# Graph and expert layers on one core: counts clamped by a tensor_scalar with a column of constants, one-hots made in pieces of four chunks

## What is computed

```
H   = l2_normalize_rows(layernorm(x))
XW  = H @ W_gcn
src, dst = edges and one self loop for each node
deg = segment_sum(ones, dst);  dinv = rsqrt(maximum(deg, 1e-30))
z_local  = segment_sum(XW[src] * (dinv[src] * dinv[dst])[:, None], dst) + b_gcn
z_global = 0.1 / n * (H @ (H.T @ H) @ W_V)
x = x + l2_normalize_rows(relu(z_local + z_global))
```

## Time and profile before

| what | us |
|---|---|
| median of 3 timed runs (5673.95 to 5677.72) | 5675.14 |
| the profiled execution, its own time | 5700.08 |
| its span, first to last instruction | 5698.0 |
| TensorE matmul busy in it | 4359.2 |
| VectorE busy | 3235.9 |
| ScalarE busy | 2114.7 |
| POOL busy | 1202.7 |

### The profile page before, as it was taken

One profiled execution on the slowest core, in us unless ns is written; L12 is line 12 of the kernel. 1 busy time (PEld: TensorE's weight loads), 2 busy tenths in 40 slices (PEclk: granted clock), 3 DMA queues, 4 the chain that ended last, 5 costly groups with the idle time before them and its releaser, 6 DMA issues. The chain is left out here.

```text
span 5698.0 us, 58897 instructions
## 1 busy us (share of the span) xinstructions
PE 4359.2 (77%) x18640; PEld 2870.1 (50%) x18640; DVE 3235.9 (57%) x6106; ACT 2114.7 (37%) x4158; POOL 1202.7 (21%) x1467
## 2 busy tenths in 40 slices
PE   1447355996784988879998898998787596889477
PEld 1335244775111767767775222223576465666366
DVE  7867244114897559731115898995787245453423
ACT  0003122113783045522223887888555011111222
POOL 1566666650220001000000111110010210000142
PEclk9868777997787989979998898899898798999788
DMA  8204243116443745320001443443453235462276
GB/s 351 103 1 162 93 134 88 39 38 208 158 155 113 241 167 196 117 45 0 0 0 58 157 156 124 165 159 94 164 191 128 88 109 177 148 199 90 107 221 203
DMA packets 460063, 733.30 MB, mean 129 GB/s; under 512 B 114081, under 2 KB 258974, under 8 KB 453004
## 3 DMA queue, kind: packets, MB, share of 16 engines
q1 hardware_dynamic: 410012, 690.18, 36.8%
q0 software_dynamic: 30096, 19.30, 1.2%
q10 hardware_dynamic: 19680, 20.48, 1.1%
HBM read 587.26 MB, written 147.21 MB: 129 GB/s over the span
## 5 line engine op out<-in xcount | busy, mean ns | idle before, releaser
L1459 PE MATMUL l2g_a_agg_acc<-all_x,l2g_a_h 128*65 128x512 f32 (+1 forms) x1400 | 644.3, 585 | 23.8 <-ACT l2g_a_agg_flat L1484 21.1
L429 POOL DMA_INDIRECT table<-first_count,first_cell x416 | 449.0, 1079 | 385.9 <-DVE first_cell L377 148.8
L1556 DVE SCALAR_TENSOR_TENSOR all_x<-all_x,l2g_a_agg_counts 128x512 f32<-128x512 f32 (+1 forms) x700 | 404.6, 625 | 121.6 <-ACT all_x L1507 121.0
L1496 ACT ACTIVATE l2g_a_agg_z<-l2g_a_agg_z 128x512 f32<-128x512 f32 (+1 forms) x700 | 344.3, 538 | 141.1 <-PE l2g_a_agg_z L1439 115.8
L1507 ACT ACTIVATE all_x<-l2g_a_agg_z 128x512 f32<-128x512 f32 (+1 forms) x700 | 353.7, 569 | 0.1
L2039 DVE SCALAR_TENSOR_TENSOR all_x<-l1f_moe_py,l1f_gate,all_x 128x256 f32 x200 | 96.7, 483 | 442.5 <-PE l1f_moe_py L1996 442.5
L892 PE MATMUL l3g_agg_acc<-l3g_agg_halves,l3g_agg_exact 128*128 128x512 f32 x1250 | 304.4, 398 | 51.6 <-DVE l3g_agg_exact L945 46.6
L1459 PEld LDWEIGHTS l2g_a_agg_acc<-all_x,l2g_a_h 128*65 128x65 f32 x1400 | 169.3, 144 | 285.9 <-issue 206.1
L1690 PE MATMUL l1g_gat_agg_acc<-l1g_gat_h,l1g_gat_agg_p 128*128 128x257 f32 x1250 | 284.8, 388 | 21.1 <-DVE l1g_gat_agg_p L1777 14.2
L1690 PE MATMUL l2g_b_agg_acc<-l2g_b_h,l2g_b_agg_p 128*128 128x257 f32 x1250 | 283.3, 387 | 19.6 <-DVE l2g_b_agg_p L1777 12.8
L2023 ACT ACTIVATE l1f_moe_hid<-l1f_moe_ph,l1f_vec 128x640 f32<-128x640 f32 x160 | 141.3, 883 | 420.9 <-PE l1f_moe_ph L2010 420.9
(11 more groups left out here) (790 smaller groups left out, 9264.8 us busy)
## 6 DMA issues: line engine op xcount, KB each, us to landing
l3g_agg_counts<-table SPq DMA_DIRECT2D x250, 320.0 KB, 3.4
l2g_a_agg_counts<-table SPq DMA_DIRECT2D x300, 256.0 KB, 4.4
table<-counting_eye_rows SPq DMA_DIRECT2D x25, 1600.0 KB, 37.3
l0g_agg_counts<-table SPq DMA_DIRECT2D x125, 320.0 KB
l1g_agg_counts<-table SPq DMA_DIRECT2D x125, 320.0 KB, 3.4
l2g_a_mask<-far SPq DMA_DIRECT2D x50, 800.0 KB, 4.4
l1g_gat_agg_counts<-table SPq DMA_DIRECT2D x150, 256.0 KB, 3.9
l2g_b_agg_counts<-table SPq DMA_DIRECT2D x150, 256.0 KB
```

Source lines behind the costliest of these rows:

```text
L429: pool.indirect_dma_start(self.table, bass.IndirectOffsetOnAxis(ap=self.cell[:, b, p:p + 1], axis=0), self.count(b, p), None, bounds_check ...
L1459: pe.matmul(to, rhs(t, r * per + h), p[:, u % n_p, 0:n], start=(t == 0), stop=(t == nt - 1), skip_group_check=True).then_inc(summed, 1)
L1496: act.activation(z[:, u % nz, 0:n], z[:, u % nz, 0:n], ACT.Relu, scale=1.0 - SLOPE).then_inc(bent, 1)
L1556: dve.scalar_tensor_tensor(out=w, in0=w, scalar=1.0, in1=counts[:, b % n_counts, 0:n], op0=ALU.min, op1=ALU.mult).then_inc(weighted, 1)
```

## The change

The clamp of parts one to five becomes a tensor_scalar whose two scalar operands are both the column `c.whole`, filled with 4096 on POOL in the first stage. Each one-hot of a slice is made by eight tensor_tensors over four chunks each (`PIECE`); only the last one of a slice carries the semaphore. Nothing else is changed.

```diff
 class InDegrees:
-    SLICE, LOW, EARLY = 32, P // 2, 8
+    SLICE, PIECE, LOW, EARLY = 32, 4, P // 2, 8
...
+    def dve_hot(self, dve, to, value, lanes):
+        n = self.SLICE
+        for k in range(0, n, self.PIECE):
+            last = dve.tensor_tensor(to[:, k:k + self.PIECE, :], over_last(value[:, k:k + self.PIECE], lanes),
+                                     over_mid(self.lane[:, 0:lanes], self.PIECE), ALU.is_equal)
+        return last
+
     def dve_high(self, dve, i):
-        n = self.SLICE
-        return dve.tensor_tensor(self.high_hot(i), over_last(self.high[:, i * n:(i + 1) * n], 2 * T),
-                                 over_mid(self.lane[:, 0:2 * T], n), ALU.is_equal)
+        return self.dve_hot(dve, self.high_hot(i), self.high[:, i * self.SLICE:(i + 1) * self.SLICE], 2 * T)
 
     def dve_low(self, dve, i):
-        n = self.SLICE
-        return dve.tensor_tensor(self.low_hot[:, i % 2], over_last(self.low[:, i * n:(i + 1) * n], self.LOW),
-                                 over_mid(self.lane[:], n), ALU.is_equal)
+        return self.dve_hot(dve, self.low_hot[:, i % 2], self.low[:, i * self.SLICE:(i + 1) * self.SLICE], self.LOW)
...
                         if sg + 1 < len(LANDS):
-                            dve.scalar_tensor_tensor(out=exact[:, i % n_exact, :], in0=counts[:, i % n_ring, :], scalar=WHOLE,
-                                                     in1=counts[:, i % n_ring, :], op0=ALU.min, op1=ALU.min
-                                                     ).then_inc(counts_set, 1)
+                            dve.tensor_scalar(exact[:, i % n_exact, :], counts[:, i % n_ring, :], c.whole[:, 0:1],
+                                              c.whole[:, 0:1], ALU.min, ALU.min).then_inc(counts_set, 1)
...
+        c.whole = first.sb("whole", [P, 1])
...
+                pool.memset(c.whole[:], WHOLE).then_inc(groups_set, 1)
...
-                sp.wait_ge(groups_set, 8)
+                sp.wait_ge(groups_set, 9)
```

## The result

The changed kernel takes 5711.23 us (median of six runs, 5704.06 to 5716.47) against 5674.55 for the kernel before beside it (six runs, 5669.05 to 5677.72): a ratio of 1.0063 [1.0053, 1.0073], 36.7 us slower. The forecast was 31 us faster. The kernel moved the other way, by about the sum that rival C had (5709).

A forecast was written before the change was run, and what follows sets the result against it. The prediction took POOL's first-scatter chain as the bound; 14.4 us from one-hots in pieces plus 16.4 from clamps made 31 us less, from 5675.14 to 5644 us, range 5634 to 5667.

The forecast's parts named there:

- rival C: VectorE passes its hold between queued instructions without gap, each slice's pieces forming one block: 34 us slower, 5709; chance 0.07.
- What bounds the kernel: First scatter, 175 to 863 us: POOL's chain sets the pace; a microsecond off it is one off the kernel.
- The mechanism: Beside one-hots, POOL needs something VectorE holds until an instruction's end; some 0.85 us of POOL's own work follow.
- Short ones cost little: Beside 256-element tensor_tensors each POOL instruction loses 0.08 us, so one-hots in pieces leave 4 us lost, gaining 14.4 us.
- The counter-argument to rival C: Early high one-hots, with nothing between them, let POOL in at each end; 25 short ones at L1097 and L675 did too.
- The clamps: Aggregation: new clamps take 593 ns, a run of five 2.63 us; 35 meetings at 0.18 us, gain 16.4 us.
- Rival B: A clamp stops POOL's own work too, not only its start: 21 us lost there, kernel 5682 us; chance 0.06.
- rival D: Gain given back by longer landing waits or TensorE's work becoming the bound: 5665 to 5678 us; chance 0.07.
- VectorE's 13 us: One-hots in pieces cost VectorE 26 x 0.50 = 13 us more, hidden by waits, chiefly 41.04 us before part three.
- The end of the stretch: Before part six: TensorE finishes part five after 37.9 us, POOL's data come after 39, so POOL decides by 1 us.

The follow-up runs named there:

- e6: Kernel before with lane numbers copied to PSUM and clamps as tensor_tensors whose second input is a PSUM column: 5633.21 us, ratio 0.9925.
- e1: Kernel before with one-hots in pieces of four chunks, old clamps kept: 5718.20 us, ratio 1.0072.
- b2: Kernel before, unchanged, run and profiled a second time: 5671.75 us for one execution.
- e4: Kernel before with lane numbers copied to PSUM and read there by whole one-hots, old clamps: 5652.18 us, ratio 0.9961.
- e8: Kernel before with one-hots in four pieces of 8 chunks, old clamps: 5704.41 us.
- e7: Kernel before with one-hots in two pieces of 16 chunks, old clamps: 5674.03 us.
- e10: Kernel before with pieces of four chunks, old clamps, VectorE waiting for its own piece once per slice, after the seventh: 5662.28 us.
- e2: Kernel before with only the clamps changed to tensor_scalars with a column, one-hots whole: 5664.06 us, ratio 0.9982.

## Why the prediction was wrong

*What bounds the kernel* held. From e6 (837.1) to e1 (918.0), an earlier table is an earlier kernel and a later one a later kernel: against b2, the changed kernel's second scatter is 35.3 us later, and its median 36.7; e6's is 36.3 earlier, its median 41. Between single executions it need not hold: the one of before that took 5700.08 us had the earlier second scatter, and b2's of 5671.75 the later one. What follows the scatter varies too.

*The mechanism* held too, and is now shown and not only read off a pair: something of VectorE's that POOL needs, given back at an instruction's end, 0.85 us of POOL's own after it. e4 and e6 name it for one-hots and old clamps, the second SBUF input. (It isn't all that can hold POOL off: the new clamp, below, has only one tensor input.) The Trainium skill (SBUF — State Buffer, "Who interferes with whom") says of two SBUF inputs that the second comes through the read interface shared with GpSimd, and infers that descriptor generation, needing the write interface, isn't touched. The first half fits e4 and e6. The second is contradicted for the indirect DMAs of this kernel, by 1.43 us in the mean (57.20 / 40) in place of 0.97 beside whole slices and by 42.49 beside pieces. They take their cells from an SBUF tile; whether it is this read that waits or the making of descriptors, no run here parts.

*The failed step is "Short ones cost little"*, the 0.08 us for each POOL instruction beside pieces, from which came 4 us of residual loss and the gain of 14.4 us. It was a loss of 38.7 us. The 0.08 us were read beside L1097, from six instructions. The first came 0.80 us after VectorE's run began at 450.50, with its landing wait mostly over by then, and the others followed 0.30 us apart:

```profile
451.30 1.14 POOL L429 DMA_INDIRECT table<-first_count,first_cell  x1 [2.02 <-DMA table<-first_count,first_cell]
452.74 1.04 POOL L429 DMA_INDIRECT table<-first_count,first_cell  x1 [0.30 <-issue]
```

e8 shows that such a chain is let in, and that a POOL instruction that comes back from its landing wait in the middle of a run isn't; POOL has one such wait after every eight instructions, and beside 17.82 and 46 us of pieces it could not be missed. At 0.28 us a piece even a close chain was shut out (227.71). A mean over one lucky chain was taken for a price per instruction. The row that spoke against it was quoted: 4.77 us at 472.29, a POOL instruction that sat out L1115 and five clamps. It was given to a rival with 0.07.

*The counter-argument to rival C was wrong in kind.* "The early high one-hots have nothing between them either, and let POOL in" is true of instructions of 1.75 us, and by e7 of 0.90; it doesn't carry to 0.28. And *rival C* had the direction and, by luck, the number. It priced blocks of one slice (13 us at the one-hots, 21 at the clamps). The loss was 38.7 us, nearly all in two blocks that ran on across the ends of slices, and at the clamps there was a gain. Neither the semaphores raised after the later slices nor VectorE's waits there for TensorE, already met, let POOL in; a wait for VectorE's own result did (e10).

*The clamps* came out as forecast in size: 609 ns (593 forecast), 2.69 us for a tight run of five (2.63), 18.8 us won in e2 where 16.4 were forecast. Rival B's price is excluded: once in, POOL was not stopped. But the new clamp does hold POOL off until its end, as the old one did:

```profile
476.32 1.20 POOL L429 DMA_INDIRECT table<-first_count,first_cell  x1 [2.02 <-DMA table<-first_count,first_cell]
```

```profile
474.49 2.70 DVE L1108 TENSOR_SCALAR l0g_agg_exact<-l0g_agg_counts,first_whole 128x640 fp32r<-128x640 f32 x5 [1.05 <-PE l0g_agg_pt L1076]
```

This is e2. The clamps end 0.53 us apart, the fourth at 476.67, and POOL's instruction ends 0.85 us later. In that trace 38 POOL instructions have a clamp under way 0.12 us after their start, which is when an undisturbed one has its 0.85 us before it. All 16 that find 0.34 us or less of the clamp left last longer by that remainder or more (to 0.02 us); 20 of the 22 that find 0.40 us or more left last 0.97. The 38 lose some 0.1 us each, where the prediction's sum took 35 meetings at 0.18. By the same count e6's clamps meet 50 POOL instructions and delay none. So the tensor_scalar is cheap because it is short, and not because it leaves POOL alone.

Yet e2 is 10 us faster, not 19: its idle time of 245.9 us sits between 237.1 and 248.7 of two executions of before, so noise of that size covers the rest, and how much of it is rival D's isn't settled.

*VectorE's 13 us* were right and covered (81.77 us of idleness before part three). *The end of the stretch* seems to have given back 8 us: from the second scatter's start to the aggregation's end it is 37.1 us before and 28.4 after. But it is 29.9 in b2, so this was a trait of the one profiled execution, and the 37.9 us that the prediction set against POOL's 39 came from the same.

**Open.** Why a run of short instructions shuts POOL out isn't known. Counting VectorE's instructions fits most of what was seen beside one-hots and L1097: POOL is let in when fewer than about four instructions have gone by since it last got in, 2.4 in e8, 1.16 / 0.34 = 3.4 at L1097 and L675, 2.87 / 0.90 = 3.2 across a landing wait in e7; it is shut out at 1.16 / 0.28 = 4.2 (227.71) and above. That is a reading of rows and no experiment of its own; e1's instruction at 227.53 got in at about the same count. The clamps don't follow it: at 472.29 POOL came 0.30 us after its last instruction, which is less than two clamps after it had got in, and sat out six instructions. In the changed kernel one POOL instruction got in between L1099 and the clamps behind it (454.07), another sat out the rest of a tight run of five (2.73 us at 473.83). POOL's idle time, 237 to 254 us in these profiles, has a part that follows no edit here. Not tried: L1099 with its second input in PSUM.

## What to carry to other kernels

Where GpSimd issues indirect DMAs beside VectorE, look for VectorE's instructions with two SBUF inputs, and put one input into PSUM if it is a constant or small (here 41 us of 5674), even at a slower instruction. Splitting them finer isn't a way to let GpSimd in; if they must be short, have VectorE wait for its own result now and then (once in eight did here). A tensor_scalar on SBUF data held GpSimd off too, but for its shorter time. And read a price per instruction from its longest as well as its mean: one row of 4.77 us, in stretches whose mean is 1.13, pointed at the result.

## What the runs showed of the hardware that was not expected

- A gapless run of short two-input VectorE instructions (0.28 to 0.61 us apart) kept one indirect DMA of GpSimd waiting up to 44.09 us, to 0.85 us past the run's end; one-hot pieces of 0.90 us and more never did. Clamps 0.73 us apart did it for up to six instructions in a row (4.77 us).
- Pieces of 0.49 us let GpSimd through when it asked again 0.30 us after its last instruction, and those of 0.49 and 0.61 us did not when it came 2.0 us after it (1.15 against 3.32 and 36.60 us in e8).
- VectorE's wait for its own result, once in eight pieces, costs 19.05 instead of 17.82 us for 64 pieces and frees GpSimd all but entirely. A semaphore that it only raises doesn't, nor does a wait for TensorE that is already met (42.49 us ran across both).
- A tensor_scalar with two per-partition scalars, 609 ns for 640 elements, cost GpSimd 4.1 us over 115 of them (e2), where the scalar_tensor_tensor of 817 ns cost 22.9. The Trainium skill (SBUF — State Buffer, "Who interferes with whom") says that a tensor_scalar in a two-port mode blocks GpSimd for the whole instruction. Whether these run in one isn't shown; in e2 a POOL instruction that came in time went through in 0.97 us, and one that came after the clamp's first 0.2 us or so waited to its end.
